# The list of expert pairs begins at its third pair and ends with its first two, and the last pair's scatters do not wait for those in front

## The reference

```
q, v = xn @ Wq, xn @ Wv
states: s_t = sigmoid(beta) * s_(t-1) + v_t        # a scan along the sequence
y = layernorm(q * states) * ln_g + ln_b
s = (y * silu(xn @ Wg)) @ Wo

logits = xn @ router.T                             # 8 experts
top_vals, top_idx = top_k(logits, 2); gates = softmax(top_vals)
for each expert e: h = xn @ w_in[e].T; a, b = split(h)
                   acc += gate_e * ((silu(a) * b) @ w_out[e].T)
g = silu(acc + bias)

out = x + s * g
```

## Time and profile before

| | us |
|---|---|
| median of 3 runs | 479.88 (479.77 to 481.7) |
| the profiled execution's own time | 481.92 |
| its span, first to last instruction | 480.1 |
| TensorE busy in the span | 408.8 (85%) |
| VectorE | 304.5 (63%) |
| GpSimd | 285.5 (59%) |
| ScalarE | 215.2 (45%) |

### The profile page before, as it was taken

The page is one execution under the profiler, slowest core; times in us unless marked ns, Lnnn a source line. Parts: engine busy times, 40 slices in busy tenths (PEclk is TensorE's granted clock), DMA queues, the critical chain, the costliest instruction groups (busy, mean ns, idle before and its releaser), DMA issues.

```text
span 480.1 us, 11839 instructions
## 1 busy us (share of the span) xinstructions
PE 408.8 (85%) x3304; PEld 325.4 (68%) x3305; DVE 304.5 (63%) x619; ACT 215.2 (45%) x340; POOL 285.5 (59%) x504
## 2 busy tenths in 40 slices
PE   0757697999999999999999999999999998999000
PEld 0544354566667988888888888888888655788000
DVE  3898979777775776766666666546464443554066
ACT  3881053466666655454545454434333222332051
POOL 4725678777851246757777757657575643266432
PEclk9999699899999999999999999999999999999655
DMA  8891543733344199999897967575679855653599
GB/s 263 239 300 57 181 171 132 262 128 132 128 139 107 39 206 249 187 153 186 166 174 161 171 116 131 78 119 83 116 127 162 132 80 109 109 59 34 88 327 372
DMA packets 90815, 74.12 MB, mean 154 GB/s; under 512 B 52880, under 2 KB 82576, under 8 KB 90768
## 3 DMA queue, kind: packets, MB, share of 16 engines
q1 hardware_dynamic: 75824, 54.86, 45.0%
q0 software_dynamic: 13296, 17.83, 22.6%
q10 hardware_dynamic: 1664, 1.06, 0.7%
HBM read 40.00 MB, written 28.74 MB: 143 GB/s over the span
## 4 chain that ended last, share of the span: by engine, by line
PE 58%; DVE 14%; DMA 9%; POOL 7%; issue 7%; ACT 3%; SPq 2%; DVEq 0%; POOLq 0%; ACTq 0%
PE bankA L1242 19%; PE bankB L1242 19%; PE bankD L1242 16%; POOL slots_dram L547 5%; DMA rows_raw<-rows_raw 3%; PE bankC L1242 2%; DMA w_raw<-x_in 2%; DMA y_dram<-rows_raw 2%; POOL stat L511 1%; PE bankD L1341 1%; DMA w_raw<-y_dram 1%; DVE work L1068 1%; DVE bn L851 1%; DVE w_raw L1227 1%; DVE rows_raw L1140 1%
## 5 line engine op out<-in xcount | busy, mean ns | idle before, releaser
L620 POOL DMA_INDIRECT y_dram<-rows_raw x64 | 105.2, 1643 | 26.3 <-issue 26.0
L1242 PE MATMUL bankD<-w_raw,rows_raw 128*128 x852 | 99.4, 273 | 0.3 <-DVE rows_raw L1144 0.3
L1242 PEld LDWEIGHTS bankD<-w_raw,rows_raw 128*128 128x128 f16 x852 | 83.0, 98 | 12.0 <-issue 0.5
L1242 PE MATMUL bankA<-rows_raw,w_raw 128*128 128x256 f16 x768 | 89.1, 273 | 1.4 <-DMA rows_raw<-rows_raw 1.3
L1242 PE MATMUL bankB<-rows_raw,w_raw 128*128 128x256 f16 x768 | 89.1, 273 | 0.0
L547 POOL DMA_INDIRECT slots_dram<-rows_raw,pos_i x64 | 68.0, 1063 | 28.2 <-issue 18.3
L1242 PEld LDWEIGHTS bankA<-rows_raw,w_raw 128*128 x768 | 74.5, 98 | 11.4 <-issue 2.5
L1242 PEld LDWEIGHTS bankB<-rows_raw,w_raw 128*128 x768 | 75.1, 98 | 8.8
L1144 DVE TENSOR_TENSOR rows_raw<-rows_raw 128x512 f16<-128x512 f32 x64 | 44.6, 696 | 45.2 <-ACT rows_raw L777 44.5
L777 ACT ACTIVATE rows_raw<-rows_raw 128x512 f16<-128x512 f32 x64 | 40.3, 630 | 51.6 <-DVE rows_raw L1140 51.6
L1140 DVE SCALAR_TENSOR_TENSOR rows_raw<-rows_raw,bankA 128x512 f32<-128x512 f32 x32 | 22.0, 687 | 55.8 <-ACT rows_raw L772 55.8
(11 more groups left out here) (199 smaller groups left out, 643.0 us busy)
## 6 DMA issues: line engine op xcount, KB each, us to landing
work<-w_exp_in SPq DMA_DIRECT2D x24, 512.0 KB, 3.8
rows_raw<-slots_dram SPq DMA_DIRECT2D x32, 256.0 KB, 3.2
w_raw<-x_in SPq DMA_DIRECT2D x9, 512.0 KB, 4.4
y_dram<-bias_in SPq DMA_DIRECT2D x4, 1024.0 KB, 11.6
w_raw<-y_dram SPq DMA_DIRECT2D x8, 512.0 KB, 7.0
out<-w_raw SPq DMA_DIRECT2D x8, 512.0 KB, 5.1
work<-x_in SPq DMA_DIRECT2D x7, 512.0 KB, 4.3
slots_dram<-fill SPq DMA_DIRECT2D x9, 260.0 KB, 2.8
```

The costliest lines, as they stand in the source:

```text
L620: pool.indirect_dma_start(out=y_dram, out_offset=bass.IndirectOffsetOnAxis(to, 0), in_=ones_y[:, b - FIRST_ONE, :] if ones else ys[i][:, s ...
L1242: last = pe.matmul(out_ap, lhsT, rhs, start=(n == 0), stop=(n == len(todo) - 1))
```

## The change

The list of pairs is read with an offset of 2: `listed(b)` gives entry (pair + 2) modulo 32 for a pair, and so blocks 0 to 27 take the pairs 2 to 29, blocks 35 and 36 the pairs 30 and 31, and blocks 37 and 38 the pairs 0 and 1. The pairs 0 to 3 are all of the first expert whatever the input, as the largest of 8 experts has at least four pairs. So blocks 37 and 38 hold different tokens, and the last block's scatters no longer wait for those of block 37. TensorE's wait for weight pieces counts two more, since block b now works on pair b + 2, and its loop with that wait ends two blocks earlier.

```
+LAST_PAIRS = 2
...
 def listed(b):
 
-    return PAIRS + b - FIRST_ONE if is_one(b) else pair_no(b)
+    if is_one(b):
+        return PAIRS + b - FIRST_ONE
+    return (pair_no(b) + LAST_PAIRS) % PAIRS if isinstance(b, int) else b + LAST_PAIRS
...
                 if first:
                     pool.wait_ge(y_started, 16 * (NT // (2 * TPC) + 1))
-                else:
+                elif not isinstance(b, int) or b < BLOCKS - 1:
                     pool.wait_ge(y_scattered[1 - i], 16 * scatters_other(b, i))
...
-            with pe.Fori(2, LAST_PIECE_BLOCK + 3, 2) as b:
+            with pe.Fori(2, LAST_PIECE_BLOCK + 1, 2) as b:
                 for j in range(2):
-                    pe.wait_ge(w_lo_ready, b + (j + PER_EXPERT))
+                    pe.wait_ge(w_lo_ready, b + (j + LAST_PAIRS + PER_EXPERT))
                     one_block(b + j, j)
             pe.wait_ge(w_lo_ready, PIECES)
-            with pe.Fori(LAST_PIECE_BLOCK + 4, FIRST_ONE - 3, 2) as b:
+            with pe.Fori(LAST_PIECE_BLOCK + 2, FIRST_ONE - 3, 2) as b:
```

## The result

The changed kernel took 479.95 us in the median of 20 runs (477.56 to 481.88), and the kernel before, run beside it, 482.53 us in the median of 20 (479.77 to 484.63). The ratio is 0.9943, with a 95% interval from 0.9922 to 0.9964: 0.57% less time, where 0.56% was forecast. The predicted time, 477.2 us, and the range, 476.3 to 479.2, were both too low. The gain was forecast right, the level that it was taken from was not: three runs of before had given 479.88 us, twenty gave 482.53. That the ratio is met to 0.01% is luck, as its interval is 0.42% wide.

What follows compares the result with a forecast made beforehand. The prediction took the end to be bound by GpSimd's row of scatters, where the last block waits for block 37's. Removing 2.67 us and adding 0 took the 479.88 us median to 477.2 us, range 476.3 to 479.2.

Steps and rivals of the forecast that it cites:

- the last of the sum: Whole kernel: 2.67 us taken off 479.88 us, the median of three runs, giving 477.2 us, 0.56% less.
- The wait that goes: Last block on GpSimd: line 617 starts 0.08 us after its cast, not after block 37's landing, 2.67 us earlier.
- What the earlier scatter meets: Last block's scatters: bursts start after block 37's bytes end, so the second's landing stays at 3.87 us.
- Rival 1: Last scatters land slower behind block 37's, in 4.49 us for example, cutting the gain to 2.05 us; chance 18%.
- The Trainium skill's rule: Last scatter: about 2.0 us fixed cost, mostly behind the last byte, making the gain 4.2 us; rival's chance 4%.
- The stronger wait for weights: TensorE at blocks 2 to 19: needed piece arrives early, 4.2 us to spare at block 5; cost 0.
- the prediction's signs of being wrong: Landing over 4.2 us, line 617 idle over 0.5 us, or TensorE idle at line 1245 between blocks 2 and 19.
- rival 2: TensorE before blocks 2 to 19: the raised weight wait binds, 3.8 us a block, up to 69 us; chance 3%.
- The renumbered pairs and SyncE's two instructions: Block loops: renumbering costs 0; SyncE's extra register instructions, 0.34 us in all, are hidden.
- The chances: Whole kernel: 62% faster, 35% no change, 3% slower, with the line for faster at 477.48 us.

Runs made afterwards that it cites:

- The two experiments that do one half each: List renumbered and weight wait raised, last block's scatter wait kept: 0.9991; or only that scatter wait removed from the kernel before: 0.9957.
- the two repeats: The changed kernel run again unaltered, twice, each against the kernel before: ratios 0.9967 and 0.9951.
- one weight piece more: Changed kernel with TensorE waiting at blocks 2 to 17 for one more weight piece: 554.58 us in one run.
- third time: The changed kernel, unaltered, in its third set of runs against the kernel before: ratio 0.9951.
- scatter wait off only: Kernel before, with its old list, without the last block's wait for block 37's scatters: ratio to before 0.9957.
- wait between the last scatters: Changed kernel with the last block's second scatter waiting for its first to land: ratio to before 1.0013.
- cast ahead: Changed kernel with the last block's destination cast moved before block 37's scatters and a small add removed: ratio to before 0.9937.

## Why the prediction was right or wrong

**The step that failed is the last of the sum:** "The wait is a fixed piece at the end, so I take it off the median: 477.2 us". That the wait is a fixed piece was right. The median of three runs was not the kernel's level: it lay 2.3 to 2.7 us below the medians of 17 to 35 runs, about as much as the whole gain. 482.53 - 2.67 = 479.86 would have met the 479.95. The sum's own basis, the profiled execution, gave 481.92 - 2.67 = 479.25, 0.7 us off; that a single execution lay near the level is luck too. The range had 0.7 us for the scatter of the runs; the three runs shown, from 479.77 to 481.7, already spread over 1.9.

**The wait that goes: right.** Line 620 was released by the cast, 0.08 us after its end, the gap taken from two other small instructions. The first issue came 0.70 us later and the second 1.87 (0.71 and 1.87 expected). Together the stretch shrank by 2.74 us (2.67). The two experiments that do one half each put all of it on the wait.

**What the earlier scatter meets: right.** The bursts did not overlap, the landing took 3.80 us (3.87). Rival 1, a landing that gives part back, did not come up in any of six profiles with the wait off; their landings are 3.70 to 3.86 us.

**The Trainium skill's rule** on the fixed cost of a GpSimd DMA ("DMA: Bandwidth & Descriptors", "Anatomy of one DMA — SWDGE (gpsimd) path") would have given an estimated 4.2 us of gain; the stretch shows 2.74. The trace after disagrees as the one before did: 450.94 - 448.91 = 2.0 us pass before the first byte, and the landing at 454.58 comes 0.4 us after the last burst's end (mark 35, 454.19).

**The stronger wait for weights: right, and the margin is real.** In the changed profile block 5's offset is read at 192.9 us and its piece is done at 187.09 + 1.22 = 188.31: 4.6 us to spare (4.2 expected).

```profile
187.09 1.22 DVE L1061 SCALAR_TENSOR_TENSOR w_raw<-work,w_raw 128x1024 f32 x1
```

```profile
L1361 PEldq TENSOR_LOAD <-blk_off x2: 298/300/301, 190.8 to 192.9; - x2
```

One of the prediction's signs of being wrong did come up by its words, idle time at line 1245 between blocks 2 and 19:

```profile
186.56 2.81 PE L1245 MATMUL bankA<-rows_raw,w_raw 128*128 128x256 f16 x24 [0.40 <-DMA rows_raw<-rows_raw]
```

It is the one such time, at block 4, and a transpose of rows ended it, not a weight piece. The kernel before has the same at block 3:

```profile
177.74 2.79 PE L1242 MATMUL bankA<-rows_raw,w_raw 128*128 128x256 f16 x24 [0.38 <-DMA rows_raw<-rows_raw]
```

So the sign should have named what ends the idle time. The price in rival 2 was off in two ways: I had 3.8 us a block for the next piece; it was 55.9 / 17 = 3.3 us of idle time over the 17 blocks that were held, and 16.9 / 17 = 1.0 us for the clock, which was not in it.

**The renumbered pairs and SyncE's two instructions: no cost to be seen**, 0.9991 with an interval across 1.

**The chances.** The forecast lay 0.27 us beyond the line for "faster" (0.5%); the measured 0.57% lies beyond it too, but the interval (0.36 to 0.78%) holds that line, and the two repeats came out at 0.33 and 0.49%. So the change is worth about half a per cent, and by times alone it stays open on which side of that line.

## What to carry to other kernels

A wait that stands on the chain after the last compute is worth its idle time in full, less what is late next on the same engine; read that from the engine's own timeline. Here the sum for this stretch came out to a tenth of a microsecond. A small gain must be stated as a ratio, or taken off a level from many runs: three runs of a kernel whose runs spread over 5 us can miss the level by as much as the gain. And where a count in a wait is raised, find out by the order of the producer's rounds whether the next count would bind: here it was the last free one.

## What the runs showed of the hardware that had not been expected

- Where the 5 us of scatter sit: over the ten profiles of before, after and the experiments but "one weight piece more", the last group of matmuls starts between 441.57 and 442.80 us (from block 2 on, TensorE's idle times ahead of it were ended by transposes of rows by DMA, 0.2 to 1.4 us each, but for two of 0.2 and 0.3 us), one profile has the 1.4 us of late scatters, and from the first load of y to the end 23.6 (third time) to 25.3 us (scatter wait off only) pass. Together about 4 us. These ranges overlap for kernels with and without the wait; what makes a transfer late in one execution and not in the next was not looked into.
- The scatter that waited for a landing was issued 1.09 us after that landing (wait between the last scatters, seen once), while scatters that follow another issue come 0.30 us after its end (cast ahead, three times).
- After an idle time of TensorE of 3 to 3.4 us the first group of 24 matmuls took 2.79 us in 6 cases, at a granted clock of 1.00, and 4.07 to 4.48 in 10, at 0.61 to 0.67, which is a mixture of the two levels, 1.2 and 2.4 GHz; where the groups behind it were looked at they ran at 1.00 again. Where the clock fell, the stall cost half as much again as its own length.
